# PEER stage: turning and summing the four heads' weights with matmuls in transpose mode instead of products with the identity

## What is computed

```python
x = x + _L3_attn_ref(_layernorm(x), ...)
x = x + _L3_ffn_ref(_layernorm(x), ...)          # the last block of all

def _L3_ffn_ref(hidden_states, W_up, W_down, W_q, keys, down_embed, up_embed):
    # B, T, H = 8, 256, 128; 4 heads; 512 experts; 64 keys; K = 8
    sim = ...                                     # query . keys, per head and half
    ...                                           # top 8 x top 8, again top 8: indices, scores
    de = down_embed[indices]
    ue = up_embed[indices]
    w = silu(einsum('btd,bthkd->bthk', hidden_states, de) * softmax(scores))
    experts_states = einsum('bthk,bthkd->btd', w, ue)
    dense = einsum('bti,di->btd', silu(einsum('btd,id->bti', hidden_states, W_up)), W_down)
    return dense + experts_states
```

## Time and profile before

| | |
|---|---|
| time, median of 3 runs | 1815.65 us (1812.27 to 1816.45) |
| span of the profiled execution | 1807.1 us (its device time is not listed apart) |
| PE (TensorE matmuls) busy | 1480.0 us, 82%, 9545 records |
| DVE busy | 1436.8 us, 80% |
| ACT busy | 1338.4 us, 74% |
| POOL busy | 1210.7 us, 67% |
| mean granted TensorE clock | 0.897 of 2.4 GHz |
| L1768 on PE | 512 records, 90.0 us |

### The profile page before, as it was taken

One profiled execution on the slowest core, in us unless ns is written; L12 is line 12 of the kernel. 1 busy time (PEld: TensorE's weight loads), 2 busy tenths in 40 slices (PEclk: granted clock), 3 DMA queues, 4 the chain that ended last, 5 costly groups with the idle time before them and its releaser, 6 DMA issues.

```text
span 1807.1 us, 27511 instructions
## 1 busy us (share of the span) xinstructions
PE 1480.0 (82%) x9545; PEld 1061.4 (59%) x9545; DVE 1436.8 (80%) x2200; ACT 1338.4 (74%) x2742; POOL 1210.7 (67%) x999
## 2 busy tenths in 40 slices
PE   5677677667899996676879999689899977899975
PEld 2343333345677775444557777566677755677854
DVE  4679999999988899889998778887998998611154
ACT  4468657757998887786788878798998887744453
POOL 4148659876777688886667667887778978800055
PEclk9678768778999998687999999899999988899987
DMA  5023412523443542221444543242544513122200
GB/s 198 1 71 72 117 39 82 117 71 107 128 135 95 173 117 58 71 71 39 117 119 127 147 121 93 59 137 72 162 106 136 158 47 92 47 83 74 99 1 6
DMA packets 84585, 170.10 MB, mean 94 GB/s; under 512 B 9440, under 2 KB 14944, under 8 KB 84064
## 3 DMA queue, kind: packets, MB, share of 16 engines
q1 hardware_dynamic: 84448, 168.36, 33.4%
HBM read 99.11 MB, written 2.10 MB: 56 GB/s over the span
## 4 chain that ended last, share of the span: by engine, by line
PE 46%; DVE 21%; ACT 17%; POOL 8%; issue 5%; DMA 2%; SPq 0%; DVEq 0%; POOLq 0%; ACTq 0%
DVE m L1052 9%; ACT m L1027 5%; PE ps L1444 5%; PE ps L966 5%; PE ps L1456 5%; DVE dtuB L1044 4%; ACT L345 4%; PE ps L1081 3%; PE ps L1183 3%; PE ps L1315 3%; POOL o L1670 2%; POOL o L1665 2%; PE ps L713 2%; ACT o L670 2%; PE ps L700 2%
## 5 line engine op out<-in xcount | busy, mean ns | idle before, releaser
L1062 POOL TENSOR_TENSOR m<-m 128x1024 f32<-128x1024 f32 x256 | 768.9, 3008 | 84.8 <-DVE m L1052 84.4
L1052 DVE TENSOR_TENSOR_SCAN m<-m,dtuB 128x1024 f32<-128x1024 f32 x256 | 584.9, 2285 | 18.6 <-ACT m L1027 5.6
L1027 ACT ACTIVATE m<-m,Aneg 128x255 f32<-128x255 f32 x1024 | 427.6, 497 | 24.5 <-DMA m<-m 23.2
L1044 DVE TENSOR_TENSOR dtuB<-m 128x1024 f32<-128x1024 f32 x256 | 342.5, 1338 | 13.1 <-DMA m<-m 5.0
L345 ACT ACT_TABLE_LOAD x188 | 241.2, 1283 | 3.3
L362 POOL TENSOR_TENSOR o<-o,mhalf 128x2 f32<-128x2 f32 x64 | 19.7, 308 | 222.1 <-DVE o L356 222.1
L1081 PE MATMUL ps<-m,w_const 128*32 128x256 f32 x2048 | 148.7, 415 | 5.7 <-POOL m L1062 5.7
L1425 ACT ACTIVATE o<-ps,w_mo 128x256 f32<-128x256 f32 x256 | 106.2, 471 | 51.0 <-PE ps L1448 50.9
L1444 PE MATMUL ps<-o 128*128 128x256 f32 x512 | 138.2, 392 | 6.8 <-ACT o L1425 5.2
L966 PE MATMUL ps<-m,wc 128*128 128x256 f32 x512 | 136.2, 425 | 6.2 <-ACT m L383 6.2
L1456 PEld LDWEIGHTS ps<-o 128*128 128x128 f32 x1024 | 128.6, 191 | 16.3 <-issue 4.9
(11 more groups left out here) (246 smaller groups left out, 2783.8 us busy)
## 6 DMA issues: line engine op xcount, KB each, us to landing
m<-m SPq DMA_DIRECT2D x256, 256.0 KB, 4.9
m<-spread SPq DMA_DIRECT2D x64, 512.0 KB, 5.0
o<-in_mox SPq DMA_DIRECT2D x128, 256.0 KB, 3.4
o<-in_l1x SPq DMA_DIRECT2D x88, 256.0 KB, 2.9
w_mb<-in_mb SPq DMA_DIRECT2D x1, 2288.0 KB, 12.1
m<-in_cwr SPq DMA_DIRECT2D x1, 2048.0 KB, 16.0
w_l3f<-in_l3f SPq DMA_DIRECT2D x1, 1536.0 KB, 17.4
X<-in_x SPq DMA_DIRECT2D x4, 256.0 KB, 7.2
```

The source lines that it names most:

```text
L1027: op = e.activation(dA[at % NA][:, j, 1:CH], R[q][:, h * CH + 1:h * CH + CH], ACT.Exp, scale=Aneg[:, l, 4 * g + j:4 * g + j + 1])
L1044: e.tensor_tensor(dtuB[:, :, :], bc(R[q][:, (2 + h) * CH:(3 + h) * CH].unsqueeze(1), 4, CH), Br[k % 2], ALU.mult).then_inc(S.dve, n.tick(f ...
L1052: e.tensor_tensor_scan(flat(G[at % NG]), flat(dA[at % NA]), flat(dtuB[:, :, :]), 0.0, ALU.mult, ALU.add).then_inc(S.dve, n.tick(f"s{g}"))
L1062: e.tensor_tensor(G[at % NG], G[at % NG], Cr[k % 2], ALU.mult).then_inc(S.pool, n.tick(f"c{g}"))
```

## The change

The 16 products per half (four heads, four blocks) become matmuls in transpose mode. Operands, bank, `start` and `stop` flags, waits and semaphores stay.

```diff
                         for k in range(4):
-                            op = e.matmul(a[:, cut(k)], v.Em[h % 2][:, cut(k)], ident, start=h == 0 and k == 0, stop=h == 3,
+                            op = e.matmul(a[:, cut(k)], v.Em[h % 2][:, cut(k)], ident, is_transpose=True, start=h == 0 and k == 0, stop=h == 3,
                                           skip_group_check=True)
```

## The result

The changed kernel takes 1821.32 us (median of 20 runs, 1812.97 to 1827.26), the kernel before 1814.99 us (20 runs, 1808.75 to 1821.49). The ratio is 1.0031, with a 95% interval of 1.0015 to 1.0046: slower by 0.3%, a little over the 0.2% that I had called the limit of what can be told. The forecast was 1816.5 us and no measurable change. The time lies within the range, and the likeliest case was the wrong one: the case next to it, "the clock takes more than is gained", came out. Two runs, one of 3947 us of the kernel before and one of 2507 us of the fifth experiment, lie far from all others and are left out throughout.

A forecast was written before the change was run, and what follows sets the result against it. No engine bounds the whole; TensorE alone bounds 1585 to 1720 us, and the last 87 us are steps waiting on each other. 1815.65 - 7.2 (direct gain) + 8 (clock) gives about 1816.5 us, range 1807 to 1824.

The forecast's parts named there:

- the likeliest case: Whole kernel: direct gain and clock's cost cancel to within 3.6 us, about 1816.5 us, no measurable change; chance 44%.
- the clock takes more than is gained: Rival 2, 22%: late rises, at 1538.9 us and in the last 87 us, cost up to 14 us; 1822.5 us.
- The records: L1768 goes from 512 to 256 records; groups take 0.6 to 0.7 us at 2.4 GHz, 1.2 at 1.2 GHz.
- The sum, +0.8 us: Whole kernel: direct gain of 7.2 us against a clock's cost of 8 us, added to 1815.65 us.
- The direct gain, 7.2 us: Shorter L1768 groups on the chain: 3.9 us before 1585 us plus 3.3 us in the end, at an unchanged clock.
- The end's part, 3.3 us: Last 87 us, the two last PEER stages: shorter groups on the chain win 1.6 + 0.46 + 0.9 + 0.3 us.
- The other part, 3.9 us: Before 1585 us: 12 groups on the chain win at most 7.7 us, of which half was taken.
- The clock's term, +8 us: Five clock rises come 3.4 to 6.8 us later, costing 0.8 to 3 us each, 4 to 14 for all.
- The rises: Clock rises near 791, 1177, 1539, 1774 and 1802 us follow stretches filled by L1768; half-emptied, they rise later.
- The clock holds: Rival, 20%: other matmuls keep the rises where they are, leaving the direct gain alone, 1808.4 us.
- Transposes count for nothing: Rival, 10%: transposes do not count towards a clock rise, costing about 4 us more than the sum; 1820.5 us.
- The change does nothing: Rival, 4%: the adding transpose keeps two records a product in L1768; 1815.7 us.

The follow-up runs named there:

- run 5: Kernel before, products kept, plus four zero transposes ahead of each group's wait; ratio 1.0017 (0.9995 to 1.0038) against the kernel before.
- run 6: Changed kernel, all groups in transpose mode, plus eight zero transposes ahead of each group in chunks 6 and 7 alone; ratio 0.9999 against the kernel before.
- run 7: Kernel before, all groups as products, plus eight zero transposes ahead of each group in chunks 6 and 7 alone; ratio 0.9979 against the kernel before.
- run 8: Changed kernel plus zero transposes ahead of each group, four in chunks 0 to 5, eight in the last two; 1811.66 us, 0.9979 against the kernel before.
- run 9: Kernel before, with transpose mode and eight zero transposes ahead of each group in the last two chunks alone; 1810.56 us, ratio 0.9978.
- run 3: Changed kernel plus four zero transposes ahead of each group's wait, all chunks; ratio 0.9988 (0.9972 to 1.0004) against the kernel before.
- run 10: Kernel before with transpose mode in chunks 4 and 5 alone, products elsewhere; ratio 0.9993 (0.9974 to 1.0013) against the kernel before.
- run 2: Kernel before with transpose mode in chunks 0 to 5 alone, products in the last two; ratio 1.0026 (1.0007 to 1.0045) against the kernel before.
- run 1: Kernel before with transpose mode in chunks 6 and 7 alone, products in the other six; ratio 0.9998 (0.9980 to 1.0016) against the kernel before.

## Why the prediction was right and wrong

**The records.** Right. 256 records, 0.63 and 1.1 us a group; the whole change in the record count is 9545 to 9289 as written.

**The sum, +0.8 us.** The measured ratio makes +5.6 us, 2.7 to 8.3 by its interval. The sum was too low by about 4.8 us (1.9 to 7.5): either the direct gain was counted too high or the clock's cost too low. The runs do not settle which.

**The direct gain, 7.2 us.** Each group is shorter as written; how much of that reaches the end of the program is what no run isolates. The end's part, 3.3 us, fits the 2.9 us between runs 6 and 7, but run 8 does not repeat it, and the 3.5 us of run 9 against before hold a higher clock as well (0.91 for 0.81). The other part, 3.9 us, was half of the chain's 7.7 us of L1768 in the scan's part. That half was a guess about what is late next, and no run shows it. Run 3, near the clock of before with all the shorter groups, is 2.2 us under before, which suggests a small gain, about 2 to 3 us. But its fillers may hide some of it. Run 5 differs from run 3 in nothing but the form of the groups, and transpose mode is 5.3 us faster there (0.9988 against 1.0017, error about 5 us), at a clock that is 0.013 lower; between runs 6 and 7, in the same way, it is 3.6 us slower (error about 5 us) at 0.014 lower. With the clock's difference priced at 4.5 to 5.1 us per 0.01 (below), the first pair gives a gain of about 11 us and the second of about 3, each an estimate with an error of 5 us and more. A gain of 7.2 us is excluded by neither.

**The clock's term, +8 us.** Right in kind. Within each kernel the runs with a lower clock tend to be the slower ones; over all runs that list a clock, each kernel's against its own mean, 0.01 of mean clock goes with 4.5 to 5.1 us, by whether the runs of the kernel before are counted. The change takes 0.013 to 0.016, which makes an estimate of 6 to 8 us. With a gain of 2 to 3 us that sums to the measured +5.6 us within its error. But this is a correlation, and run 5, with 0.012 more clock and no gain in time, shows its limit; with a gain of 7.2 us the clock's cost would be 12.8 us, which lies in my 4 to 14 as well. That the clock costs time is shown by run 6 against the change and run 7 against before, where work was added in the end stretch alone, and borne out by runs 3 and 8.

**The rises.** I had five of them follow bursts of L1768. The last one, at 1801.7 us, is gone, and L1774 lost 0.9 us, as written. The one at 1539 us came later: L1768's eight records at 1541 us leave the clock low, and the matmuls of L1167 behind them still take 1.06 us for two records at 1543 us. But my second rival's place, that this rise and its long stretch carry the loss, fell with run 10: chunks 4 and 5 alone cost nothing that shows (0.9993, up to 1.0013). No single place has been found that carries the loss.

```profile
1541.14 2.24 PE L1768 MATMUL ps<-w_const,o 128*128 128x128 f32 x8
1543.17 1.06 PE L1167 MATMUL ps<-o 128*128 128x256 f32 x2
...
1545.44 0.59 PE L1168 MATMUL ps<-o 128*128 128x256 f32 x2
```

**The rivals.** "The clock holds" (1808.4 us) is out: 0.877 for 0.893. "Transposes count for nothing" is out by run 3, where transposes alone brought the clock back. "The change does nothing" is out by the record count. Rival 2, the clock takes more than is gained, is what came out, and it had 22% against 44% for the forecast. Its tipping point was a clock's cost over 10.8 us against a gain of 7.2; whether the cost was that high or the gain smaller is the question left open above. That the order of the shared queues falls badly, whatever the clock, was not among my rivals; run 2, with 0.008 off the clock where that rival allowed 0.005, speaks against it, but in the scan's part no run excludes it.

**The marks.** I had written that a mean clock between 0.87 and 0.897 goes with the forecast. It was 0.881 in the profile and 0.877 over the runs, and the time was still slower: a mean clock within these marks does not tell "no change" from "slower".

## What to carry to other kernels

When an edit makes TensorE's work shorter in a stretch where it waits for others, ask what its clock does there: list the places where the clock rises and what filled the time before them, and count an edit that halves this filling as a possible loss for the matmuls behind it. Here time was won back by giving the waiting TensorE harmless work where little else of the kernel stands behind it (the last stages: run 7, 0.2% under before); in all stages of the kernel before it won nothing (run 5). A share of the chain is an upper bound of a gain. And before a cause is read from the lengths of two profiles, look how far two profiles of the same instructions lie apart.

## What the runs showed of the hardware that was not expected

- A float32 matmul in transpose mode with `start=False` adds to what the bank holds, at the price of a plain transpose: four in 0.63 us at 2.4 GHz.
- Matmuls with a zero operand lift the clock too: 128 records of zeros more in the end stretch took it from 0.70 (the change) to 0.91 (run 6).
- Float32 transposes lift it about as products do: a mean of 0.892 with transposes as fillers, 0.889 with products.
- The same program has a mean clock that differs from run to run (0.869 to 0.884 for the changed kernel), and with it a time that differs by up to 14 us. Stretches of the same instructions differ by 3.9 us in 87 (runs 8 and 9) and by 10.7 us in 900 (before and run 1). A change of a few us in such a kernel is not to be read from one profile.
